# Reordering TensorE, ScalarE and VectorE queues in a Fourier-layer stage and an attention stage

## The chip, the cores and the metric

The kernel runs on one core of a Trainium2 chip. The metric is the device time of one execution in microseconds (us); lower is better. All data is fp32. Engines are called PE (TensorE; PEld is its weight load), DVE (VectorE), ACT (ScalarE), POOL (GpSimd) and SP (the queue that issues most DMAs).

## What is computed

64 images of 64 x 64 x 3 go through a Fourier neural operator, and 64 sequences of 77 text tokens through an embedding; both give rows of 64 numbers, 141 rows for each item. Then come local attention and a two-layer expert MLP over these rows. Cut to what matters:

```python
h = layer_norm(x @ fc0_w + fc0_b, ln0_g, ln0_b)          # 32 channels per pixel
for i in range(4):                                       # four Fourier layers
    x1 = spectral_conv(h, w1, w2)     # rfft2, 12 x 24 modes mixed over channels, irfft2
    x2 = einsum('bchw,oc->bohw', h, conv_w[i]) + conv_b[i]
    h = layer_norm(x1 + x2, ln_g[i], ln_b[i])
    if i < 3: h = gelu(h)
h = gelu(h @ fc1_w + fc1_b); h = gelu(h @ fc2_w + fc2_b); h = h @ fc3_w + fc3_b
h = concatenate([h[..., 0], text_embedding(x_txt)], axis=1)       # 64 + 77 rows of 64
h = h + attention(layernorm(h))        # 8 heads of 8, a 7 x 7 local mask, softmax
h = h + experts(layernorm(h))          # relu MLP, two layers, one of 16 experts by route_id
```

## The kernel before, in words

The images are taken as 32 pairs. `token_network` has a stem (about the first 500 us), three inner layers that run inside a hardware loop over `s` (about 553 to 1038, 1090 to 1590 and 1630 to 2130 us) and a last layer with the heads (to about 3010 us). `attention_and_experts` takes the last 620 us. Each engine has its own program, written out in the order of the source. Engines meet only at semaphores, and an engine waits where its program says so, with everything behind that wait queued.

**Inner layers** (`layer(s)` of each engine). A pair `g` has two halves `h`, and each half two units `u`. On PE, `step(g)` works on up to three pairs at once:

- `widen(s, 0, g, h)` (L479, two matmuls of 512 columns) starts the PSUM banks of half `h` with the inverse transform; it waits for the spectrum copies `zb` of DVE and ACT and for the bank to be read out (`norm_ready`).
- `conv(s, 0, g, h)` (L496, 32 matmuls) adds the 1 x 1 convolution; its end lets ACT square (`square`, L772), DVE sum the squares (`reduce`, L1073), POOL raise them to the power -1/2 (`rstds`, L1296), DVE scale, multiply and add (`normalise` L1087, `gain` L1121, `bias` L1128) and ACT apply gelu (`gelu`, L784, into `hp`).
- `turn(s, 0, g, h, k)` (L546, four transposes of `hp`), copied out by ACT's `hc_copy` (L796) into `ho`, which SP stores.
- `f1(s, 0, g, j)` (L571, 32 matmuls, j = 0 to 3) is the forward transform along x. It writes one PSUM bank, which ACT's `a_copy` (L812) must empty before the next `f1`. `f1` with j = 0 waits for all four gelus of its pair. `f2` (L585) is the transform along y, and ACT's `x_copy` reads it.
- `i1(s, g + 1, first, end)` (L507) is the inverse transform along y of the next pair, in three pieces of 24, 20 and 20 matmuls. Its result is copied by DVE and ACT (`z_copy`, L1133 and L817) into `zb`, for the next `widen`.

PE's loop body is one pair and runs 31 times in each layer; ACT's and DVE's loop bodies hold two pairs, with `even` and `odd` for the two halves. In PE's body before, `widen` of half 0 stands first, so the end of the loop lies between the last `f1` and it, and `f1` with j = 0 follows the second `conv`. In ACT's `odd`, the two squares stand ahead of the four `a_copy`.

**Attention.** A pair has three blocks b = 0, 1, 2, and `step(i, p, b)` of each engine works on up to four pairs. DVE adds the mask to the scores (`with_mask`, L1821), takes the maximum (`row_max`, L1831), POOL subtracts it (`shift`, L1930), ACT takes the exponential (`exp`, L1713), and PE transposes (`turn`, L1581) and multiplies with the values (`values`, L1594). Around it run two layer norms: `norm` (DVE) and `power` (POOL), and `norm_end` (DVE, L1804), the product with the reciprocal deviation: `xn` for the attention's norm of the next pair, `yn` for the experts' norm of the pair before the last. PE transposes `yn` in `back_y` (L1621), ACT copies it (`yT_copy`, L1727), and `exp` is behind `yT_copy` in ACT's queue. POOL's `with_bias` (L1937) writes `h1b`. All of it is at b = 0 of DVE's step:

```python
                if here:
                    with_mask(i, p, b)
                if b == 0 and nxt:
                    norm1_end(*nxt[0:2])
                if here:
                    row_max(i, p, b)
                if b == 0 and (c := at(i, p, 0, 9)):
                    final(*c[0:2])
                if b == 0 and old:
                    norm_end(yn, rs2, rs2_ready, yn_ready, num(old[0], old[1]))
```

Of the kernel before, what the change touches and what calls it, by code (L numbers as in the profile page):

```python
# [25 lines left out]
PAIRS = IMGS // 2  # L26
# [58 lines left out]
def token_network(nc, t, tokens):  # L85


    with ExitStack() as ctx:
# [361 lines left out]
        def _(pe):  # L450
# [157 lines left out]
            def layer(s):  # L608

                def where_older(g):  # L610
                    return nullcontext() if isinstance(g, int) else pe.If(g >= 2)
# [4 lines left out]
                def step(g):  # L616
                    edge = isinstance(g, int)
                    here = not edge or g < PAIRS
                    old, older = not edge or 1 <= g <= PAIRS, not edge or g >= 2
                    if here:  # L620
                        widen(s, 0, g, 0)
                    if older:
                        with where_older(g):
                            turn(s, 0, g - 2, 1, 0)
                    if here:
                        conv(s, 0, g, 0)
                    if older:
                        with where_older(g):
                            turn(s, 0, g - 2, 1, 1)
                            f2(s, 0, g - 2, 0)  # L630
                    if old:
                        turn(s, 0, g - 1, 0, 0)
                    if older:
                        with where_older(g):
                            f2(s, 0, g - 2, 1)
                    if old:
                        turn(s, 0, g - 1, 0, 1)

                    if here:
                        widen(s, 0, g, 1)  # L640
                        conv(s, 0, g, 1)
                    for j, piece in enumerate(((0, 6), (6, 11), (11, 16), None)):
                        if old:
                            f1(s, 0, g - 1, j)
                        if here and piece:
                            with where_next(g):
                                i1(s, g + 1, *piece)
                step(0)
                with pe.Fori(1, PAIRS) as g:
                    step(g)  # L650
# [108 lines left out]
        def _(act):  # L759
# [98 lines left out]
            def layer(s):  # L858
                def even(i, p):
                    here, old, older, nxt = (where(i, p, 0, lag) for lag in (0, 2, 4, -2))  # L860
                    if older:
                        hc_copy(s, older[0], 1, 0)
                    if here:
                        square(s, here[0], 0, 0)
                    if older:
# [15 lines left out]

                def odd(i, p):
                    here, old, nxt = (where(i, p, 0, lag) for lag in (0, 2, -2))
                    if here:
                        square(s, here[0], 1, 0)
                        square(s, here[0], 1, 1)
                    if old:
                        for j in range(4):
                            if j == 3 and nxt:
                                z_copy(s, nxt[0])  # L890
                            a_copy(s, 0, old[0], j)
                    elif nxt:
                        z_copy(s, nxt[0])
                    if here:
                        gelu(s, here[0], 0, 0)
                        gelu(s, here[0], 0, 1)
# [464 lines left out]
def attention_and_experts(nc, t, tokens, out):  # L1361

    with ExitStack() as ctx:
# [122 lines left out]
        def num(i, p):  # L1486
            return 2 * i + p
# [284 lines left out]
        def _(dve):  # L1772
# [109 lines left out]
            def step(i, p, b):  # L1882
                here, prev, old = at(i, p, 0, 0), at(i, p, 0, 3), at(i, p, 0, 6)
                nxt, nxt2 = here and at(i, p, 0, -3), here and at(i, p, 0, -6)
                if here:
                    with_mask(i, p, b)
                if b == 0 and nxt:
                    norm1_end(*nxt[0:2])
                if here:
                    row_max(i, p, b)  # L1890
                if b == 0 and (c := at(i, p, 0, 9)):
                    final(*c[0:2])
                if b == 0 and old:
                    norm_end(yn, rs2, rs2_ready, yn_ready, num(old[0], old[1]))
                if b == 0 and prev:
                    o_norm(*prev[0:2])
                if b == 1 and prev:
# [178 lines left out]
```

## Time and profile before

| | us |
|---|---|
| median of 3 runs | 3648.15 |
| the 3 runs | 3648.17, 3635.49, 3648.15 |
| profiled execution, its time | 3639.14 |
| profiled execution, its span | 3637.3 |
| PE busy | 3132.9 (86%) |
| DVE busy | 2467.3 (68%) |
| ACT busy | 2218.8 (61%) |
| POOL busy | 2127.3 (58%) |
| granted TensorE clock, mean | 0.933 |

The span is the time from the first to the last instruction of the profiled execution; 1.8 us of that execution's time lie around it. The three runs differ by 13 us among themselves, and the profiled one lies between them. The busy shares are means over stages with different limits; for the change only the inner layers and the attention matter.

### The profile page before, as it was taken

The numbers are of one execution on the slowest core, as the hardware profiler recorded it, in microseconds if no ns is written. First come the engines' busy times: TensorE is split into PE (matmuls) and PEld (weight loads), VectorE is DVE, ScalarE is ACT, GpSimd is POOL, SyncE is SP. The second block draws the span as 40 slices with busy tenths as digits, with TensorE's granted clock in tenths as the row PEclk, the third lists the DMA queues.
The fourth block names the chain that finished last, engine by engine and source line by source line (L and its number), as shares of the span: only waits on it lengthen the run. The fifth ranks groups of instructions, "written<-read, shape, count | busy, mean of one in ns | idle before, by whom it ended". The sixth has DMA issues, their size and how long they took to land. (4 is left out here: it accounts for less than half of the span.)

```text
span 3637.3 us, 202203 instructions
## 1 busy us (share of the span) xinstructions
PE 3132.9 (86%) x86496; PEld 2151.1 (59%) x86496; DVE 2467.3 (68%) x3756; ACT 2218.8 (61%) x3645; POOL 2127.3 (58%) x1147
## 2 busy tenths in 40 slices
PE   6777777999968999968999958999999986999998
PEld 3555556777756777756777753333333334666666
DVE  6665547888847888847888844444444436999996
ACT  4455445777745777746777736777777773555554
POOL 2322216888847888838888834444444434555554
PEclk8888887999988999979999978999999997999998
DMA  2232234555544556545555641211121111000000
GB/s 83 94 93 93 88 128 131 169 168 168 172 149 135 169 174 171 171 137 146 168 168 172 174 133 47 60 56 52 54 58 54 54 28 41 13 12 12 12 12 9
DMA packets 206411, 366.15 MB, mean 101 GB/s; under 512 B 107186, under 2 KB 124146, under 8 KB 206018
## 3 DMA queue, kind: packets, MB, share of 16 engines
q1 hardware_dynamic: 194610, 350.25, 32.5%
q10 hardware_dynamic: 7920, 10.03, 0.9%
q0 software_dynamic: 3744, 3.84, 0.7%
q8 instruction: 110, 1.80, 0.2%
q14 instruction: 27, 0.22, 0.0%
HBM read 206.31 MB, written 157.71 MB: 100 GB/s over the span
## 5 line engine op out<-in xcount | busy, mean ns | idle before, releaser
L1296 POOL TENSOR_TENSOR rstd<-var,mhalf 128x16 f32<-128x16 f32 x512 | 1537.4, 3018 | 773.9 <-DVE var L1073 767.2
L571 PE MATMUL ps<-d,hp 128*32 128x48 f32 x32768 | 492.9, 211 | 89.7 <-ACT asb L812 41.7
L571 PEld LDWEIGHTS ps<-d,hp 128*32 128x32 f32 x32768 | 410.2, 112 | 207.6 <-issue 106.3
L1073 DVE TENSOR_REDUCE var<-sq 128x16 f32<-128x528 f32 x384 | 402.8, 1050 | 146.3 <-ACT sq L772 146.2
L812 ACT COPY asb<-ps 128x384 f32<-128x384 f32 x512 | 254.3, 497 | 386.9 <-PE ps L571 264.8
L1087 DVE TENSOR_TENSOR zt<-ps,rstd 128x512 f32<-128x512 f32 x512 | 351.4, 686 | 200.0 <-POOL rstd L1296 195.5
L546 PE MATMUL ps<-ident,hp 128*128 128x128 f32 x2048 | 377.9, 309 | 12.7 <-ACT ho L796 10.0
L496 PEld LDWEIGHTS ps<-cwl,hc 64*64 64x64 f32 x16384 | 273.4, 139 | 146.9 <-issue 136.3
L772 ACT ACTIVATE sq<-ps 128x512 f32<-128x512 f32 x512 | 288.0, 599 | 115.4 <-PE ps L496 81.7
L507 PEld LDWEIGHTS ps<-dyi,gt 64*48 64x48 f32 x16384 | 234.7, 125 | 202.0 <-issue 190.0
L479 PE MATMUL ps<-zb,ex 48*128 48x512 f32 x1024 | 303.5, 668 | 53.8 <-issue 34.8
L507 PE MATMUL ps<-dyi,gt 64*48 64x32 f32 x16384 | 277.2, 212 | 80.7 <-ACT gt L836 36.4
L546 PEld LDWEIGHTS ps<-ident,hp 128*128 128x128 f32 x2048 | 275.7, 197 | 110.3 <-issue 79.2
L1073 DVE TENSOR_REDUCE var<-sql 128x16 f32<-128x528 f32 x128 | 141.2, 1105 | 262.4 <-ACT sql L772 262.4
L496 PE MATMUL ps<-cwl,hc 64*64 64x64 f32 x16384 | 309.2, 226 | 0.0
L920 ACT ACTIVATE a<-ps,fc1b 128x1024 f32<-128x1024 f32 x256 | 271.3, 1111 | 61.1 <-PE ps L689 61.1
L585 PE MATMUL ps<-cy,asb 128*64 128x24 f32 x6144 | 253.1, 222 | 58.2 <-issue 57.4
L705 PE MATMUL ps<-a,fc 128*64 128x512 f32 x1024 | 260.9, 619 | 18.4 <-ACT a L920 18.4
L585 PEld LDWEIGHTS ps<-cy,asb 128*64 128x64 f32 x6144 | 220.0, 143 | 95.7 <-issue 69.9
L1121 DVE TENSOR_TENSOR zt<-zt,gbx 128x512 f32<-128x512 f32 x384 | 264.9, 690 | 10.2
L1128 DVE TENSOR_TENSOR zt<-zt,gbx 128x512 f32<-128x512 f32 x384 | 264.7, 689 | 10.3
L796 ACT COPY ho<-ps 128x512 f32<-128x512 f32 x384 | 223.5, 582 | 72.5 <-PE ps L546 72.5
(171 smaller groups left out, 4881.3 us busy)
## 6 DMA issues: line engine op xcount, KB each, us to landing
h_scratch<-ho SPq DMA_DIRECT2D x256, 512.0 KB
hc<-h_scratch SPq DMA_DIRECT2D x256, 512.0 KB, 4.4
wsb<-in_w SPq DMA_DIRECT2D x64, 288.0 KB
gin<-g_scratch SPq DMA_DIRECT2D x252, 72.0 KB
gin<-g_scratch SPq DMA_DIRECT2D x504, 36.0 KB
g_scratch<-hp SPq DMA_DIRECT2D x32, 192.0 KB, 3.4
g_scratch<-hp ACTq DMA_DIRECT2D x32, 192.0 KB, 4.1
tokens<-wsb SPq DMA_DIRECT2D x256, 4.0 KB
```

Source lines behind the costliest of these rows:

```text
L479: nc.tensor.matmul(main_ps(s, h, u), ex[k], zb[b][k, h, :], start=True, stop=False, skip_group_check=True, tile_position=(64 * u, 0))
L496: last = nc.tensor.matmul(main_ps(s, h, u)[64 * m:64 * m + 64, r:512:8], hc[b][k, 8 * h + r, 64 * m:64 * m + 64], cwl[k], start=False, sto ...
L507: last = nc.tensor.matmul(z[c][64 * u:64 * u + 2 * TRIG, 32 * col:32 * col + 32], gt[b][rows, k].rearrange("k n s a -> k (n s a)"), dyi[ro ...
L546: last = nc.tensor.transpose(t_mid[:, 128 * a:128 * a + 128], src, ident[:])
L571: last = nc.tensor.matmul(a_ps[row:row + 32, 2 * TRIG * k:2 * TRIG * k + 2 * TRIG], hp[b][:, u, 8 * j + k].rearrange("p v r -> p (v r)"), ...
L585: last = nc.tensor.matmul(x_ps[64 * c:64 * c + 64, o:o + KY], asb[b][:, KX * m + 2 * a + c].rearrange("y c s -> y (c s)"), cy[:], start=Tr ...
L772: nc.scalar.activation(dst, main_ps(s, h, u).rearrange("p (v n) -> p v n", v=2), ACT.Square).then_inc(sq_ready, 1)
L920: nc.scalar.activation(a1[:, 2 * u:2 * u + 2, :], f1_ps[:, 2 * u:2 * u + 2, :], ACT.Gelu, bias=fc1b[:]).then_inc(a1_ready, 1)
L1073: nc.vector.tensor_reduce(dst, src, axis=AX.X, op=ALU.add).then_inc(var_ready, 1)
L1087: nc.vector.tensor_tensor(by_px(zt[h][:, u]), by_px(main_ps(s, h, u)), scale, ALU.mult).then_inc(norm_ready, 1)
L1121: nc.vector.tensor_tensor(z, z, channels(s, 0).unsqueeze(2).to_broadcast([128, C, 16]), ALU.mult).then_inc(gain_ready, 1)
L1296: nc.gpsimd.tensor_tensor(rstd[u][:], var[u][:], mhalf[:], ALU.pow).then_inc(rstd_ready, 1)
```

## The change

It moves instructions and removes none. In PE's layer step, `widen` of half 0 goes to the end of the body, for the next pair (for pair 0 it is issued ahead of the loop); `f1` with j = 0 goes ahead of the second `conv`; the first transpose of half 1 (`turn(.., 1, 0)`) goes from the next step to a place ahead of the last `f1`. ACT follows: the first `a_copy` ahead of the squares of half 1, `z_copy` and `hc_copy(.., 1, 0)` ahead of the last `a_copy`. In the attention, DVE's product `yn` goes from behind the maximum of block 0 to right behind the mask.

```diff
--- before.py
+++ after.py
@@ -618,11 +618,6 @@
                     here = not edge or g < PAIRS
                     old, older = not edge or 1 <= g <= PAIRS, not edge or g >= 2
                     if here:
-                        widen(s, 0, g, 0)
-                    if older:
-                        with where_older(g):
-                            turn(s, 0, g - 2, 1, 0)
-                    if here:
                         conv(s, 0, g, 0)
                     if older:
                         with where_older(g):
@@ -638,13 +633,23 @@
 
                     if here:
                         widen(s, 0, g, 1)
+                    if old:
+                        f1(s, 0, g - 1, 0)
+                    if here:
                         conv(s, 0, g, 1)
-                    for j, piece in enumerate(((0, 6), (6, 11), (11, 16), None)):
-                        if old:
-                            f1(s, 0, g - 1, j)
-                        if here and piece:
+                    for j, piece in enumerate(((0, 6), (6, 11), (11, 16))):
+                        if here:
                             with where_next(g):
                                 i1(s, g + 1, *piece)
+                        if old and j == 2:
+                            turn(s, 0, g - 1, 1, 0)
+                        if old:
+                            f1(s, 0, g - 1, j + 1)
+                    if not edge or g < PAIRS - 1:
+
+                        with where_next(g):
+                            widen(s, 0, g + 1, 0)
+                widen(s, 0, 0, 0)
                 step(0)
                 with pe.Fori(1, PAIRS) as g:
                     step(g)
@@ -858,8 +863,6 @@
             def layer(s):
                 def even(i, p):
                     here, old, older, nxt = (where(i, p, 0, lag) for lag in (0, 2, 4, -2))
-                    if older:
-                        hc_copy(s, older[0], 1, 0)
                     if here:
                         square(s, here[0], 0, 0)
                     if older:
@@ -881,16 +884,19 @@
 
                 def odd(i, p):
                     here, old, nxt = (where(i, p, 0, lag) for lag in (0, 2, -2))
+                    if old:
+                        a_copy(s, 0, old[0], 0)
                     if here:
                         square(s, here[0], 1, 0)
                         square(s, here[0], 1, 1)
                     if old:
-                        for j in range(4):
-                            if j == 3 and nxt:
-                                z_copy(s, nxt[0])
-                            a_copy(s, 0, old[0], j)
-                    elif nxt:
+                        a_copy(s, 0, old[0], 1)
+                        a_copy(s, 0, old[0], 2)
+                    if nxt:
                         z_copy(s, nxt[0])
+                    if old:
+                        hc_copy(s, old[0], 1, 0)
+                        a_copy(s, 0, old[0], 3)
                     if here:
                         gelu(s, here[0], 0, 0)
                         gelu(s, here[0], 0, 1)
@@ -1884,14 +1890,14 @@
                 nxt, nxt2 = here and at(i, p, 0, -3), here and at(i, p, 0, -6)
                 if here:
                     with_mask(i, p, b)
+                if b == 0 and old:
+                    norm_end(yn, rs2, rs2_ready, yn_ready, num(old[0], old[1]))
                 if b == 0 and nxt:
                     norm1_end(*nxt[0:2])
                 if here:
                     row_max(i, p, b)
                 if b == 0 and (c := at(i, p, 0, 9)):
                     final(*c[0:2])
-                if b == 0 and old:
-                    norm_end(yn, rs2, rs2_ready, yn_ready, num(old[0], old[1]))
                 if b == 0 and prev:
                     o_norm(*prev[0:2])
                 if b == 1 and prev:
```

On PE, in the inner layers' loop body, the stretch from the second widening on, before (L479 widen, L496 conv, L571 f1, L507 i1, L546 turn):

```order
L479 MATMUL ps<-zb,ex 128x512 x2
L496 MATMUL ps<-cwl,hc 64x64 x32
L564 REGISTER_ALU
L571 MATMUL ps<-d,hp 32x48 x32
L614 COMPARE_AND_BRANCH
L515 ISA
L517 REGISTER_ALU
L507 MATMUL ps<-dyi,gt 48x32 x24
L646 UNCONDITIONAL_BRANCH
L571 MATMUL ps<-d,hp 32x48 x32
```

The same place of the changed kernel:

```order
L479 MATMUL ps<-zb,ex 128x512 x2
L564 REGISTER_ALU
L571 MATMUL ps<-d,hp 32x48 x32
L496 MATMUL ps<-cwl,hc 64x64 x32
L614 COMPARE_AND_BRANCH
L515 ISA
L517 REGISTER_ALU
L507 MATMUL ps<-dyi,gt 48x32 x24
L642 UNCONDITIONAL_BRANCH
L571 MATMUL ps<-d,hp 32x48 x32
```

The first `f1` now stands between the widening and the `conv` of half 1, and a whole `conv` and a piece of `i1` lie between it and the second `f1`.

At the end of PE's body in the changed kernel (L654 is the loop's end):

```order
L546 MATMUL ps<-ident,hp 128x128 x4
L48 REGISTER_ALU
L571 MATMUL ps<-d,hp 32x48 x32
L614 COMPARE_AND_BRANCH
L470 ISA
L476 REGISTER_ALU
L479 MATMUL ps<-zb,ex 128x512 x2
L650 UNCONDITIONAL_BRANCH
L654 REGISTER_ALU
L654 COMPARE_AND_BRANCH
```

Before, the last `f1` was followed by the loop's end; now the next pair's widening lies between them, and the transpose of half 1 ahead of them.

On DVE, block 0 in the attention's loop body, before:

```order
L1821 TENSOR_TENSOR sm<-pst,mask 128x952
L1803 ISA
L1804 TENSOR_TENSOR xn<-xn,rs 128x192
L1831 TENSOR_REDUCE mx<-sm 128x8
L1867 ISA
L48 REGISTER_ALU
L1870 TENSOR_TENSOR fin<-pst,h1b 128x192
L1803 ISA
L1804 TENSOR_TENSOR yn<-yn,rs 128x192
L1835 ISA
L1837 RECIPROCAL rden<-pst 128x24
```

The same place of the changed kernel:

```order
L1827 TENSOR_TENSOR sm<-pst,mask 128x952
L1809 ISA
L1810 TENSOR_TENSOR yn<-yn,rs 128x192
L1809 ISA
L1810 TENSOR_TENSOR xn<-xn,rs 128x192
L1837 TENSOR_REDUCE mx<-sm 128x8
L1873 ISA
L48 REGISTER_ALU
L1876 TENSOR_TENSOR fin<-pst,h1b 128x192
L1841 ISA
L1843 RECIPROCAL rden<-pst 128x24
```

The product `yn` moved ahead of `xn` and of the maximum; the final sum and the reciprocal follow the maximum directly.

## Rows read from the trace of the kernel before

**Rows 1.** Stretches: length, busy and (instructions) of each engine, PEclk, DMA share, GB/s.

```profile
800.00:1037.70 237.70, 221.99 (x9216) 175.80 (x9216) 204.12 (x281) 170.06 (x318) 210.16 (x89) 1.00 0.57 165
...
3320.00:3440.00 120.00, 108.64 (x1259) 81.98 (x1251) 110.18 (x155) 66.28 (x114) 69.31 (x65) 0.97 0.05 12
```

**Rows 2.** Waits, 800 to 1037.7 us: who for whom, total us, times, longest.

```profile
DVE var L1073 <- ACT sq L772: 21.5, 16, 2.0
...
PE ps L479 <- issue: 6.4, 16, 0.4
PE ps L571 <- ACT asb L812: 5.0, 17, 0.9
```

**Rows 3.** Timeline of PE, one pair of layer 1: start, us, what [idle before <- releaser].

```profile
710.80 0.89 PE L571 MATMUL ps<-d,hp 128*32 128x48 f32 x64
...
712.07 1.13 PE L479 MATMUL ps<-zb,ex 48*128 48x512 f32 x4 [0.39 <-issue]
...
713.78 1.16 PE L496 MATMUL ps<-cwl,hc 64*64 64x64 f32 x64
...
719.52 1.16 PE L496 MATMUL ps<-cwl,hc 64*64 64x64 f32 x64
...
720.61 0.89 PE L571 MATMUL ps<-d,hp 128*32 128x48 f32 x64
...
721.70 0.74 PE L507 MATMUL ps<-dyi,gt 64*48 64x32 f32 x48 [0.20 <-issue]
...
722.63 0.89 PE L571 MATMUL ps<-d,hp 128*32 128x48 f32 x64 [0.19 <-ACT asb L812]
...
723.45 0.65 PE L507 MATMUL ps<-dyi,gt 64*48 64x32 f32 x40
...
726.92 1.13 PE L479 MATMUL ps<-zb,ex 48*128 48x512 f32 x4 [0.39 <-issue]
```

**Rows 4.** The same timeline, DVE and ACT behind the first conv.

```profile
715.81 1.05 DVE L1073 TENSOR_REDUCE var<-sq 128x16 f32<-128x528 f32 x1 [1.64 <-ACT sq L772]
...
718.94 0.63 ACT L784 ACTIVATE hp<-zt 128x512 f32<-128x512 f32 x1 [0.44 <-DVE zt L1128]
```

**Rows 5.** Waits in the attention, 3060 to 3600 us.

```profile
PE pst L1621 <- DVE yn L1804: 40.0, 29, 1.6
...
PE pst L1570 <- DVE sm L1821: 6.0, 9, 1.8
```

**Rows 6.** Source line L1804: ns min/median/max, first and last start.

```profile
L1804 DVE TENSOR_TENSOR yn<-yn,rs x30: 341/1881/1890, 3064.4 to 3594.5; 128x192 f32<-128x192 f32 x30
```

**Rows 7.** Timeline of the attention, block 0 of one pair.

```profile
3335.93 1.14 DVE L1821 TENSOR_TENSOR sm<-pst,mask 128x952 f32<-128x952 f32 x1
...
3337.32 0.59 POOL L1937 TENSOR_TENSOR h1b<-h,bo 128x192 f32<-128x192 f32 x1
3337.38 0.74 DVE L1804 TENSOR_TENSOR xn<-xn,rs 128x192 f32<-128x192 f32 x1 [0.31 <-POOL rs L1915]
3338.05 1.13 DVE L1831 TENSOR_REDUCE mx<-sm 128x8 f32<-128x952 f32 x1
...
3338.78 1.10 PE L1594 MATMUL pst<-vv,pT 119*64 119x9 f32 x32
...
3339.26 1.78 POOL L1930 TENSOR_TENSOR sm<-sm,mx 128x952 f32<-128x952 f32 x1 [1.35 <-DVE mx L1831]
3339.37 1.88 DVE L1804 TENSOR_TENSOR yn<-yn,rs 128x192 f32<-128x192 f32 x1
...
3341.39 0.49 PE L1621 MATMUL pst<-identt,yn 128*64 128x128 f32 x3 [1.51 <-DVE yn L1804]
...
3341.92 0.47 ACT L1727 COPY yT<-pst 64x384 f32<-64x384 f32 x1 [2.64 <-PE pst L1621]
...
3342.30 1.00 ACT L1713 ACTIVATE sm<-sm 128x952 f32<-128x952 f32 x1
...
3343.34 1.13 PE L1581 MATMUL pst<-identt,sm 128*119 128x128 f32 x8
```

## The prediction

> **What bounds the kernel now.** I read the page first (busy shares, the 40 slices), then the stretches and the waits of the two stages that the change touches, then one pair of each in the timeline. In the inner layers the 16 pairs of a steady stretch take 237.70 us, 14.86 us each, with PE busy for 221.99 us, POOL for 210.16, DVE for 204.12 and ACT for 170.06 [rows 1]. PE is the bound and stands still for 15.7 us, 0.98 us a pair. That is the ceiling of any gain from order alone: 93 passes of the loop (31 in each of three layers) times 0.98 is 91 us. The waits say where it stands still: 6.4 us in 16 gaps ahead of the widening (L479), and 5.0 us in 17 gaps ahead of f1, for ACT's copy [rows 2]. In the attention PE is the bound too (108.64 of 120.00 us, DVE 110.18) [rows 1]; 40.0 us of its idle time lie in 29 waits for the product yn, 1.38 us each, and only 6.0 us in waits for the mask [rows 5]. The pair there takes 18.28 us, from the first and last start of 30 products (530.1 / 29) [rows 6].
>
> **The layers, part by part.** The matmuls are the same, so I price only gaps.
>
> (a) The widening of half 0. From the last f1 to it 712.07 - 710.80 = 1.27 us pass; from an f1 to the piece of i1 behind it, with a branch but no register wait, 723.45 - 722.63 = 0.82 [rows 3]. So 0.45 us lie in the loop's end and the widening's waits. Behind its new place there is no loop's end, but a branch and the same waits. The nearest row is the first f1 with the first i1, which has a branch and register waits too: 721.70 - 720.61 = 1.09, or 0.27 over 0.82 [rows 3]. I take 0.27 as what stays and 0.18 as the gain. The bounds are 0 (all stays) and 0.45 (nothing stays). The loop's end moves under the widening, which keeps PE busy for 1.13 us [rows 3]; I cost it at nothing, and at up to 0.45 if that cover fails. The spectrum copies it waits for get the transpose and the f1, some 1.5 us, as cover.
>
> The Trainium skill (TensorE: Matmul & The Clock Gate, the table at its head) gives PE a queue of 64 instructions. Read as a sequencer that runs far ahead, that would hide all these waits, (a) would give its full 0.45, and the sum would be 25 us better. The row speaks against it here: the first i1 starts late with "issue" as its releaser, behind an f1 of 64 records [rows 3]. I go by the row.
>
> (b) The second f1. It waits for the first a_copy, which ACT does behind two squares: 0.19 us in the pair shown [rows 3], 5.0 / 16 = 0.31 us in the mean [rows 2]. With the conv (1.09 us from its start to what follows) in between and the a_copy ahead of the squares, this wait goes. Some of the 17 gaps belong to other f1s, so I take 0.25, bounds 0.19 and 0.31.
>
> (c) Gaps at the new neighbours. The conv now stands behind an f1 and the first i1 behind the conv. The i1's 0.27 was there before; the conv's own wait may show as up to 0.27 more. I take 0, since its wait adds no register instruction in the listing.
>
> (d) A new wait. The first f1 needs all four gelus of its pair. The last starts 718.94 - 713.78 = 5.16 us after the first conv, waits for DVE, and takes 0.63 [rows 3, 4]: ready at 5.79, with some 0.05 for the semaphore 5.84. The f1 takes the old place of the second conv, 719.52 - 713.78 = 5.74 [rows 3]. Before, it came at 6.88 and had 1.04 to spare; now it is 0.10 late. I take 0.10, with 0 as the lower bound; upward it is as large as DVE is late (a rival below).
>
> What moves without a price: the second conv starts about 0.85 us later against the first. Its squares had to wait for ACT's copies anyway, and DVE's idle time ahead of the first reduce, 21.5 / 16 = 1.3 us a pair [rows 2], takes what is left. SP's loads of the half that this conv frees, and of the coefficients queued behind them, are issued as much later and are used one pair, over 13 us, later. On ACT the copy hc_copy of half 1 now stands ahead of the last a_copy and the gelus; its transpose comes before the last f1 on PE too, so ACT meets them in PE's order. POOL is busy for 13.1 us of a pair and stays under 14.5.
>
> Sum of the layers: 0.18 + 0.25 - 0.10 = 0.33 us a pair, so 93 x 0.33 = 31 us. At the upper bounds 0.45 + 0.31 = 0.76, 71 us; at the lower 0 + 0.19 - 0.10 - 0.27 = -0.18, a loss of 17 us. The edges of each layer (four passes outside the loop) I leave out.
>
> **The attention.** Before, yn starts at 3339.37, 0.11 us behind POOL's subtraction of the maximum, and lasts 1.88 us, until just after that ends; uncontended it took 0.34 at its shortest [rows 6, 7]. Its input has been ready since before the mask. Now it runs right behind the mask, at about 3337.1, beside POOL's power, an instruction of 3 numbers a row. PE's transpose (L1621) need not wait behind the values (3338.78 + 1.10 = 3339.88), so the wait of 1.51 goes [rows 7]. **Late next** is the exponential: it starts at 3342.30 because yT_copy (3341.92) stands ahead of it, though the subtraction ended at 3339.26 + 1.78 = 3341.04 [rows 7]. It will start at about 3341.1, 1.2 us sooner, and PE's next transposes (3343.34), which need it, come 1.2 us sooner as well; PE itself is there sooner still and waits some 0.3 us for it.
>
> The price is the maximum's start. It was 3338.05, behind xn, which was ready at about 3337.35 and took 0.74 beside POOL's h1b [rows 7]. yn fits into the gap of 0.31 ahead of xn, and xn ends with h1b as before, so I take 0.1 us of delay. Bounds: 0; or all of yn's 0.34 and one more h1b of 0.59, 0.93. Gain: 1.2 - 0.1 = 1.1 us a pair; between 1.2 - 0.93 = 0.27 and 1.38. With 30 products: 33 us, between 8 and 41.
>
> **The sum.** 31 + 33 = 64 us off the profiled execution's 3639.1: 3575 us. The median of the runs shown, 3648.15, is 9 us above that execution, so as a median it may come out a little higher; I say 3576.
>
> **The rivals.** 0.5% of this kernel, 18 us, is about what a measurement can tell from no change.
>
> 1. The layers give nothing, because the gelu wait and gaps at the new neighbours eat (a) and (b); for it speaks that each is no larger than 0.3. Then the attention alone gives 33: 3606 us.
>
> 2. PE's clock rises as well. In the attention the granted clock is 0.97 in the mean, against 1.00 in the steady layers [rows 1]. Of its two levels (1.2 and 2.4 GHz) that means 6% of the time at the lower, 7.2 us of 120, worth up to 3.6 us there and some 16 us over 530. The engine stood still 1.4 us in each pair before it fell. If these falls go, and the layers reach their upper half (50 us): 3639 - 33 - 16 - 50 = 3540 us. The Trainium skill (TensorE: Matmul & The Clock Gate, A second HAM failure mode: psum-queue depth-cycling) says that short idle times between groups of matmuls can make the clock oscillate; by it the falls would go. That the steady layers have idle times and no falls speaks for it only in part.
>
> 3. In the attention, yn and xn both wait for h1b, the maximum comes 0.93 late, and 8 us are left of 33: 3600 us. Against it: yn starts before h1b.
>
> 4. **Slower:** the first f1 waits for a late gelu. DVE does the last half's normalise, gain and bias behind the first reduce, and all PE's work queues behind this f1. From 0.33 + 33 / 93 = 0.68 us beyond the 0.10 on, the whole change loses. If DVE were 1.2 us late in every pair, the layers would lose 93 x 0.87 = 81 us and the total be 3639 - 33 + 81 = 3687 us. Against it: DVE is idle for 1.3 us ahead of that very reduce [rows 2, 4].
>
> 5. The change does less than it says: the product still meets a POOL instruction and the layers' gaps are refilled at once. That is within 18 us of before, say 3630.
>
> **How the numbers follow.** The forecast has 0.63, rival 1 0.15, rival 2 0.10, rival 3 0.04, rival 4 0.04, rival 5 0.04. Faster holds the forecast, rivals 2 and 3 and nearly all of rival 1: 0.90; the same 0.06; slower 0.04. The range reaches down to just below rival 2, 3538, and up past rival 1 to where the layers are at their lower bound and the attention gives its 33: 3639 + 17 - 33 = 3623.
>
> **What would show it.** Right: in a steady layer a pair takes about 14.5 us, the waits for a_copy ahead of f1 nearly vanish, the gap ahead of the widening shrinks to about 0.2, and short waits of the first f1 for gelu appear. In the attention the pair takes about 17.2 us, yn lasts 0.35, and PE's wait for it is gone, with a smaller one for the exponential in its place. Wrong: PE waits for gelu of 0.5 us or more, a gap at the second conv, or a maximum that starts 0.5 us late.

## The result and the profile after

| | before | after |
|---|---|---|
| median | 3647.64 us (4 runs, 3635.49 to 3648.17) | 3548.15 us (4 runs, 3545.62 to 3558.63) |
| profiled execution | 3639.14 us | 3549.24 us |
| its span, mean clock | 3637.3 us, 0.933 | 3547.4 us, 0.937 |

The ratio is 0.9727 (95% interval 0.9704 to 0.975): 2.7% faster, 99.5 us between the medians and 89.9 between the profiled executions. The forecast was 3576 us in a range from 3538 to 3623. The side and the range hold; the gain is larger than the 64 us of the sum.

I cut both spans at three places: the first matmul of the mix (the product of the spectrum with the layer's weights) of the first and of the fourth layer, and the start of the last matmul of the heads' second product (L705, after the change L710). The three inner layers with their mixes take 1611.6 us before (520.3 to 2131.9) and 1562.5 after (520.7 to 2083.2), **49.1 us less** (forecast 31). From that last matmul to the end it is 639.0 and 597.1, **41.9 us less** (forecast 33). The rest changes by 1 us.

The same two kinds of stretch after (columns as in [rows 1]):

```profile
800.00:1030.00 230.00, 218.09 (x9146) 173.92 (x9144) 204.45 (x278) 170.08 (x316) 206.85 (x88) 1.00 0.53 167
3240.00:3360.00 120.00, 115.77 (x1356) 87.61 (x1360) 109.18 (x171) 72.22 (x124) 76.39 (x72) 1.00 0.06 13
```

Against [rows 1], PE is busy for 94.8% of the layers' stretch instead of 93.4%, and for 96.5% of the attention's instead of 90.5%; there the granted clock is now 1.00, where it was 0.97.

**The layers.** A pair takes 14.41 us (mean of the distances between widenings two pairs apart, in eight places) against 14.87: 0.46 less, 43 of the 49.1 us over 93 passes. The other 6 lie in one place near the start of each layer. From the widening of half 1 in pair 1 to that in pair 2 it takes 23.81, 24.35 and 21.96 us in the three layers before, and 21.33, 20.72 and 21.61 after: 6.5 us less together, with a mean granted clock of 0.66, 0.72 and 0.84 there before and of 0.84 in all three after. Not all of it need come from the change: in the experiments below that have before's layers (attention alone, nine matmuls of no use, yn behind xn) the three add up to 68.9 to 72.8 us, in those that have the widening moved to 62.8 to 70.8. The waits after, 790 to 1015 us (columns as in [rows 2]):

```profile
DVE var L1079 <- ACT sq L777: 9.9, 23, 0.5
...
DVE zt L1093 <- POOL rstd L1302: 8.5, 7, 1.2
...
PE ps L571 <- ACT hp L789: 2.5, 8, 0.4
...
PE ps L479 <- DVE zb L1139: 1.9, 8, 0.3
PE ps L479 <- issue: 1.7, 8, 0.2
PEld ps L571 <- ACT asb L817: 0.5, 3, 0.2
```

PE's waits of f1 for asb [rows 2] are gone, those of the widening on "issue" fell from 6.4 us in 16 gaps to 1.7 in 8. Two new ones stand in their place, both 8 times, in every second pair: f1 for the gelu, and the widening for the spectrum's copy zb. DVE now waits up to 1.2 us for POOL's power, in every second pair too. The pairs themselves alternate between about 14.25 and 14.57 us; before, nearly all took 14.8 to 14.95.

The timeline of PE shows where each is, in a pair with these waits and in one without (columns as in [rows 3]):

```profile
698.19 1.13 PE L479 MATMUL ps<-zb,ex 48*128 48x512 f32 x4
699.63 0.89 PE L571 MATMUL ps<-d,hp 128*32 128x48 f32 x64 [0.31 <-ACT hp L789]
700.45 1.16 PE L496 MATMUL ps<-cwl,hc 64*64 64x64 f32 x64
701.66 0.74 PE L507 MATMUL ps<-dyi,gt 64*48 64x32 f32 x48
702.33 0.89 PE L571 MATMUL ps<-d,hp 128*32 128x48 f32 x64
...
705.24 0.71 PE L546 MATMUL ps<-ident,hp 128*128 128x128 f32 x4
705.88 0.89 PE L571 MATMUL ps<-d,hp 128*32 128x48 f32 x64
707.01 1.13 PE L479 MATMUL ps<-zb,ex 48*128 48x512 f32 x4 [0.25 <-DVE zb L1139]
708.07 1.16 PE L496 MATMUL ps<-cwl,hc 64*64 64x64 f32 x64
...
712.75 1.13 PE L479 MATMUL ps<-zb,ex 48*128 48x512 f32 x4
713.93 0.89 PE L571 MATMUL ps<-d,hp 128*32 128x48 f32 x64
```

The first f1 starts 1.44 us behind the widening of half 1 in one pair and 1.18 in the next, where a following matmul without a wait comes at 1.06 (707.01 to 708.07); in both it starts 0.05 us after the last gelu has ended. The conv starts 0.82 behind that f1, the first i1 1.21 behind the conv, the second f1 0.67 behind that i1. The last f1 is followed by the widening of the next pair after 1.13.

**Why every second pair.** POOL and DVE just ahead of the next late pair:

```profile
723.96 0.27 POOL L1312 TENSOR_SCALAR wmean<-wmean 128x18 f32<-128x18 f32 x1
...
724.44 1.16 POOL L1314 TENSOR_TENSOR wsb<-wsb,wmean 128x576 f32 x1 [0.20 <-POOL wmean L1312]
...
725.79 0.67 POOL L1318 TENSOR_TENSOR wsb<-wsb,sgn 128x288 f32 x1 [0.19 <-POOL wsb L1314]
...
726.05 0.95 DVE L1127 TENSOR_TENSOR zt<-zt,gbx 128x512 f32<-128x512 f32 x1
...
726.41 6.25 POOL L1302 TENSOR_TENSOR rstd<-var,mhalf 128x16 f32<-128x16 f32 x2
...
729.91 0.69 DVE L1093 TENSOR_TENSOR zt<-ps,rstd 128x512 f32<-128x512 f32 x1 [1.23 <-POOL rstd L1302]
```

Once in two pairs POOL centres the weights of a coming couple: 2.5 us in three instructions, from 723.96 to 726.46. The two powers rstd come that much later, DVE's normalise waits 1.23 us for one, and DVE's next copies, zb among them, are late. DVE's gain also takes 0.95 us beside the sign product instead of 0.69, ahead of the gelu that f1 waits for. Whether this is what PE waits for is tested below (POOL's centring taken apart).

**The attention.** The product yn after (columns as in [rows 6]):

```profile
L1810 DVE TENSOR_TENSOR yn<-yn,rs x32: 348/348/776, 3014.0 to 3529.7; 128x192 f32<-128x192 f32 x32
```

Its median falls from 1881 to 348 ns. PE's 29 waits for it [rows 5] are gone; what PE still waits for, 3060 to 3500 us, is mainly

```profile
PE pst L1576 <- DVE sm L1827: 7.0, 13, 0.6
...
PE pst L1587 <- ACT sm L1719: 3.3, 18, 0.3
```

and block 0 of one pair reads (columns as in [rows 7]):

```profile
3250.78 1.15 DVE L1827 TENSOR_TENSOR sm<-pst,mask 128x952 f32<-128x952 f32 x1 [0.23 <-issue]
...
3251.85 0.35 DVE L1810 TENSOR_TENSOR yn<-yn,rs 128x192 f32<-128x192 f32 x1
...
3252.12 0.75 DVE L1810 TENSOR_TENSOR xn<-xn,rs 128x192 f32<-128x192 f32 x1
3252.79 1.13 DVE L1837 TENSOR_REDUCE mx<-sm 128x8 f32<-128x952 f32 x1
...
3254.70 0.52 PE L1627 MATMUL pst<-identt,yn 128*64 128x128 f32 x3
...
3255.81 1.00 ACT L1719 ACTIVATE sm<-sm 128x952 f32<-128x952 f32 x1
...
3256.86 1.13 PE L1587 MATMUL pst<-identt,sm 128*119 128x128 f32 x8
```

The maximum starts 2.01 us behind the start of the mask; in the pair of [rows 7] it was 3338.05 - 3335.93 = 2.12. But the pairs alternate, 2.11 and 1.79 before and 2.01 and 2.11 after, and in the mean (21 pairs before, 23 after, 3100 to 3500 us) the maximum starts 1.96 us behind the mask before and 2.06 after: 0.10 later. From the mask to the exponential it takes 5.03 us here where [rows 7] has 6.37, in the mean 5.08 instead of 6.21, so 1.13 less. PE has no wait ahead of its transpose of yn.

### The profile page after: what moved, and what is told of

The parts are those of the page before. It is cut to its first block and busy times, and to the rows that moved or that the text cites. A ratio compares the mean times of both kernels' runs of the same rounds, so it can differ in the third digit from the quotient of the medians.

```text
span 3547.4 us, 202068 instructions
## 1 busy us (share of the span) xinstructions
PE 3109.5 (88%) x86496; PEld 2136.9 (60%) x86496; DVE 2434.8 (69%) x3756; ACT 2229.8 (63%) x3645; POOL 2121.1 (60%) x1147
## 5 line engine op out<-in xcount | busy, mean ns | idle before, releaser
L571 PEld LDWEIGHTS ps<-d,hp 128*32 128x32 f32 x32768 | 412.7, 113 | 288.9 <-issue 128.7
L571 PE MATMUL ps<-d,hp 128*32 128x48 f32 x32768 | 496.9, 212 | 100.2 <-issue 55.9
L546 PE MATMUL ps<-ident,hp 128*128 128x128 f32 x2048 | 375.1, 308 | 11.9 <-ACT ho L801 8.3
L496 PEld LDWEIGHTS ps<-cwl,hc 64*64 64x64 f32 x16384 | 272.1, 139 | 138.4 <-issue 132.2
L507 PEld LDWEIGHTS ps<-dyi,gt 64*48 64x48 f32 x16384 | 232.8, 125 | 176.6 <-issue 164.7
L479 PE MATMUL ps<-zb,ex 48*128 48x512 f32 x1024 | 300.9, 664 | 40.8 <-DVE zb L1139 31.0
L507 PE MATMUL ps<-dyi,gt 64*48 64x32 f32 x16384 | 274.8, 211 | 55.1 <-ACT gt L841 35.2
L496 PE MATMUL ps<-cwl,hc 64*64 64x64 f32 x16384 | 307.7, 226 | 0.0
L546 PEld LDWEIGHTS ps<-ident,hp 128*128 128x128 f32 x2048 | 274.3, 197 | 42.9 <-ACT ho L801 9.0
L1127 DVE TENSOR_TENSOR zt<-zt,gbx 128x512 f32<-128x512 f32 x384 | 275.9, 718 | 10.2
L789 ACT ACTIVATE hp<-zt 128x512 f32<-128x512 f32 x384 | 231.8, 627 | 80.1 <-DVE zt L1134 80.1
L710 PE MATMUL ps<-a,fc 128*64 128x512 f32 x1024 | 261.1, 619 | 18.3 <-ACT a L926 18.3
L1134 DVE TENSOR_TENSOR zt<-zt,gbx 128x512 f32<-128x512 f32 x384 | 265.0, 690 | 10.3
```

Of the source, the lines that this page charges most:

```text
L479: nc.tensor.matmul(main_ps(s, h, u), ex[k], zb[b][k, h, :], start=True, stop=False, skip_group_check=True, tile_position=(64 * u, 0))
L496: last = nc.tensor.matmul(main_ps(s, h, u)[64 * m:64 * m + 64, r:512:8], hc[b][k, 8 * h + r, 64 * m:64 * m + 64], cwl[k], start=False, sto ...
L507: last = nc.tensor.matmul(z[c][64 * u:64 * u + 2 * TRIG, 32 * col:32 * col + 32], gt[b][rows, k].rearrange("k n s a -> k (n s a)"), dyi[ro ...
L546: last = nc.tensor.transpose(t_mid[:, 128 * a:128 * a + 128], src, ident[:])
L571: last = nc.tensor.matmul(a_ps[row:row + 32, 2 * TRIG * k:2 * TRIG * k + 2 * TRIG], hp[b][:, u, 8 * j + k].rearrange("p v r -> p (v r)"), ...
L1127: nc.vector.tensor_tensor(z, z, channels(s, 0).unsqueeze(2).to_broadcast([128, C, 16]), ALU.mult).then_inc(gain_ready, 1)
```

## The experiments

The first four take the change apart. Their comparison has 10 runs of the kernel before, median 3649.22.

**The attention alone.** The two lines of yn moved behind `with_mask` in the kernel before.

> The kernel before with only DVE's product yn moved right behind the mask. The profiles of before and after put 1.30 us a pair and 42 us in all into the attention (pair 18.28 to 16.98 us). If the two parts of the change add up, this gives about 42 us (ratio 0.9885), the clock there is 1.00 instead of 0.96 to 0.97, and the layers stay at 14.86 us a pair. Rival: the parts interact, for instance the attention gains only 33 us (my forecast, order alone, no change of the clock) and the rest came with the layers: ratio 0.991.

Measured: 3599.61 us (4 runs, 3598.84 to 3604.94), ratio 0.9874 (0.9845 to 0.9902). The layers' pair is at its old 14.87 us; the attention's pairs alternate between 16.57 and 17.10, as after the whole change, and the clock is 1.00:

```profile
3150.00:3270.00 120.00, 115.83 (x1380) 87.73 (x1377) 109.27 (x172) 70.62 (x121) 75.98 (x73) 1.00 0.06 13
```

**The layers alone.** The whole change, with yn back behind `final`.

> The changed kernel with yn back behind the maximum: PE's and ACT's part alone. If the parts add up: 49 us (ratio 0.9865), a steady pair of 14.41 us, attention as before with a pair of 18.28 us and falls of the clock. Rival: 31 us, as forecast (0.9915).

Measured: 3596.39 us (4 runs, 3594.45 to 3598.19), ratio 0.9863 (0.9836 to 0.989). The layers' pair is 14.42 us; the attention's is as before, its mean clock too:

```profile
3270.00:3390.00 120.00, 108.34 (x1256) 81.75 (x1253) 109.79 (x159) 64.62 (x111) 68.50 (x67) 0.97 0.05 12
```

0.9874 times 0.9863 is 0.974, within the interval of the whole's 0.9727: no effect of one part on the other is seen, and the rise of the clock belongs to the attention's part.

**Only the first f1 ahead of the conv, its copy ahead of the squares.**

```diff
+                    if old:
+                        f1(s, 0, g - 1, 0)
                     if here:
                         conv(s, 0, g, 1)
...
+                    if old:
+                        a_copy(s, 0, old[0], 0)
                     if here:
                         square(s, here[0], 1, 0)
```

> Before, with only the first f1 ahead of the second conv and the first a_copy ahead of the squares. From the two traces: the wait for a_copy goes (0.26 us a pair), the first i1 stands behind a conv instead of an f1 (0.15 gained), and the first f1 waits for gelu (0.25 lost if the rest of the order were as after). Sum 0.16 us a pair, 15 us, ratio 0.996. In this order the first conv is as late as before, so gelu follows at the same distance (5.84 us behind the first conv) and f1 stands 5.74 behind it: the wait should be 0.10 to 0.25. Rival: the gelu wait eats the part, no gain or a loss (ratio 1.000 to 1.003), and the whole layer gain comes from the widening's part.

Measured: 3631.74 us (7 runs, 3621.13 to 3635.34), ratio 0.9947 (0.9927 to 0.9968); the pair is 14.76 us, 0.11 less. Its waits, 700 to 900 us:

```profile
PEld ps L571 <- ACT hp L787: 11.3, 13, 0.9
...
PE ps L479 <- DVE zb L1138: 8.4, 14, 0.8
...
PEld ps L571 <- ACT asb L815: 2.2, 14, 0.2
```

The waits for asb and gelu fall on PE's weight loads and are mostly hidden behind its matmuls: the first f1 starts 1.17 us behind the widening, 0.11 later than without a wait. But the widening, whose old gap stood on "issue", now waits 0.6 us for the spectrum's copy: PE reaches it earlier and DVE does not. Before, that gap was 0.4 [rows 2], so 0.2 us of what the move gains are given back there, and 0.11 at the f1.

**Only the widening moved**, with the transpose and the loop's body as in the change, f1 and a_copy as before.

> Before, with only the widening of half 0 at the end of the body and the transpose of half 1 ahead of the last f1, ACT's z_copy and hc_copy to match; the first f1 stays behind the second conv. From the two traces: 0.16 us a pair for the gap ahead of the widening and 0.11 for the transpose's neighbours, with no gelu wait: 0.27 us a pair, 25 us, ratio 0.993. Rival: the gap of 0.45 is the loop's jump and shows elsewhere (ahead of the first conv), no gain: 1.000.

Measured: 3610.88 us (4 runs, 3605.87 to 3614.69), ratio 0.9896 (0.9867 to 0.9925). The pair is 14.62 us, 0.26 less, so in the steady part this is what I expected; the time fell more. The three layers with their mixes take 1580.3 us, 31 less, where 93 x 0.26 is 24; the other 7 lie from pair 1 to pair 2 again (20.78, 20.86 and 21.17 us). The two moves by themselves give 0.11 + 0.26 = 0.37, together 0.46. A likely reason is that with the widening at the end of the body its copy has the time that the f1's move alone lacks: the widening's wait for zb is 0.6 us in every pair there, and up to 0.3 in every second pair after the whole change.

The next four ask what limits now, and what the clock was worth. Here the kernel before has 13 runs, median 3649.14.

**The clock by itself.** The kernel before with nine matmuls of no use where PE stood still for yn.

```diff
+                for n in range(9):
+                    nc.tensor.matmul(ps[:, 2, 0:128], ident[:], ident[:], start=True, stop=True)
```

> The kernel before with nine more matmuls of 128 columns on PE, ahead of the transpose that waits for yn, into a PSUM bank that is free there; their result is never read. They take about 1.1 us (eight of their kind take 1.0), so PE is busy where it stood still 1.4 us a pair, and nothing it waits for comes sooner. It asks whether the falls of the clock in the attention (0.96 to 0.97, 1.00 after the change) come from that standstill. If so: clock 1.00 there, the pairs of 19.1 us become 18.0, some 10 us less in all (ratio 0.997). Rival: the clock falls for another reason, and it stays at 0.96 to 0.97; then the pairs of 18.0 us stay or get up to 0.2 us longer (ratio 1.000 to 1.002).

Measured: 3646.27 us (10 runs, 3633.63 to 3650.06), ratio 0.9985 (0.997 to 1.0). In its attention

```profile
3120.00:3240.00 120.00, 119.73 (x1411) 94.92 (x1409) 99.04 (x162) 65.19 (x110) 68.83 (x69) 1.00 0.05 12
```

PE is busy for 99.8% of it and the clock is 1.00 with yn at its old place. But nine took 2.11 us, where I had expected 1.1, more than the gap, so pairs of 18.09 and 18.22 us show only a part of what the clock is worth, and the interval reaches up to no change. I made it again with **five**, in a set of comparisons in which every kernel took about 4.5% less (17 runs of before, median 3481.61; the last section has more on it).

> As the longer filler, with five matmuls instead of nine. Nine took 2.11 us a pair, longer than the 1.4 us of standstill, and gave a granted clock of 1.00 with pairs of 18.09 and 18.22 us; five should take 1.2 us and fit. If the standstill is what lets the clock fall, the clock is 1.00 here too and the pairs are all 17.9 to 18.0 us, none of 19.1: 30 x 0.4 = 12 us less than before, ratio 0.997, with nothing of yn's order changed. Rival: a standstill of 0.2 to 0.3 us with less work in between still lets it fall, and the mean pair stays at 18.3 to 18.4 (ratio 1.000).

Measured: 3471.2 us (12 runs, 3455.92 to 3486.0), ratio 0.9965 (0.995 to 0.998). All its pairs take 17.9 or 18.0 us, none 19.07:

```profile
3020.00:3140.00 120.00, 116.37 (x1343) 89.96 (x1343) 112.19 (x164) 64.93 (x111) 69.46 (x67) 1.00 0.05 12
```

0.35% of this kernel is 12 us (7 to 17 by the interval), and the mean of 27 pairs, 17.95 us instead of 18.41, makes 12 too: the standstill cost its own length and, on top, some 12 us through the clock.

**yn behind xn** instead of ahead of it, in the kernel before: `norm1_end`, then yn, then `row_max`.

> The kernel before with yn between xn and the maximum instead of ahead of both. My theory: the gain comes from taking yn out of POOL's subtraction, and the place ahead of xn is only the cheapest, since DVE waits there for xn's input anyway. Then yn takes 0.35 here and delays the maximum, the subtraction and the exponential by 0.35 to 0.4, against 0.1 in the change: a pair 0.25 to 0.3 us longer than after (17.25 instead of 16.98), gain 31 to 34 us of the attention's 42 (ratio about 0.990). Rival: xn's own end is set by POOL's with_bias, and yn right behind it is held as well or the delay is covered: as good as the change (0.9874) or a loss of more than 0.6 us a pair against it.

Measured: 3604.95 us (4 runs, 3599.04 to 3609.83), ratio 0.9875 (0.9849 to 0.9902); pairs of 16.54 and 16.95, mean 16.75, where I had expected 17.25. My expectation fell, and its rival (as good as the change, 0.9874) came true. The product takes 0.35 us here as well:

```profile
L1804 DVE TENSOR_TENSOR yn<-yn,rs x25: 343/346/346, 3095.0 to 3497.4; 128x192 f32<-128x192 f32 x25
```

What matters is that yn is out from under POOL's subtraction; whether it stands ahead of xn or behind it does not. Both places are ahead of the maximum; one behind it but clear of the subtraction wasn't tried.

**The conv of half 1 split around the first f1**, on the changed kernel, to give the gelu more time (the last argument of `conv` names the half of its matmuls).

```diff
+                    if here:
+                        conv(s, 0, g, 1, 0)
                     if old:
                         f1(s, 0, g - 1, 0)
                     if here:
-                        conv(s, 0, g, 1)
+                        conv(s, 0, g, 1, 1)
```

> The changed kernel with the second conv in two halves of 16 matmuls, the first f1 between them. It gives gelu 0.55 us more and keeps the first a_copy ahead of the squares. If the new wait for gelu (0.38 and 0.12 us in alternate pairs of the changed kernel, 0.25 in the mean) is a loss on PE's path, it goes: a steady pair of 14.16 to 14.2 us instead of 14.41, 20 to 23 us less than the changed kernel (ratio to before about 0.967). Rival: another engine or the spectrum's copy is late next, and the time stays within 5 us of the changed kernel (0.972): the waits ahead of the widening grow by what the f1 gains.

Measured: 3553.51 us (4 runs, 3551.97 to 3557.05), ratio 0.9741 (0.9717 to 0.9764); the pair is 14.44, no less. The wait for the gelu is gone, and the widening waits instead, up to 0.5 us where it was 0.3:

```profile
707.30 1.13 PE L479 MATMUL ps<-zb,ex 48*128 48x512 f32 x4 [0.43 <-DVE zb L1143]
```

So removing the gelu wait alone gives nothing; that both waits hang on the same late DVE is what the experiment after the next tests. The halves also cost 0.08 to 0.26 us more than the conv in one piece.

**The normalise of a new half ahead of the old half's gain on DVE**, on the changed kernel: `z_copy` one line up.

> The changed kernel with DVE's copy of the spectrum ahead of the gain of the same step instead of behind it. In the changed kernel every second widening waits 0.25 us for this copy. If that wait is on the path, 0.12 us a pair goes, 10 us in all (ratio to before 0.970). Rival: it shifts the late gain and bias onto gelu or onto the next reduce, and nothing or a little is lost (0.972 to 0.975).

Measured: 3565.69 us (4 runs, 3564.54 to 3573.25), ratio 0.9771 (0.9749 to 0.9794); the pair is 14.60, 0.19 worse, where I had expected a gain and its rival at most a small loss (0.975). Two of its waits, 790 to 1015 us:

```profile
DVE zt L1093 <- POOL rstd L1301: 15.6, 8, 2.0
PE ps L571 <- ACT hp L789: 4.5, 15, 0.4
```

A DVE that reaches its wait for POOL sooner only waits longer (15.6 us where it was 8.5), and pushes the gain behind it. That points at POOL.

**POOL's centring taken apart.** On the changed kernel, its last product (the sign) is issued one step later, between other powers (`w_sign` is that product, taken out of `w_centre`).

```diff
+                        if p == 1 and h == 0 and not final:
+                            w_sign(s, i)
```

> The changed kernel with the last of POOL's three instructions that centre the next layer's weights (the product with sgn, 0.67 us) put one step later, behind the next pair's first two powers. In the changed kernel these three delay the power of every second pair by about 1 us, DVE waits 1.2 us for it, and the spectrum's copy and the widening behind it come late. If this is what bounds the layers now, DVE's wait falls to about 0.4 us, and the steady pair goes from 14.41 to 14.3 us (the widening's wait of 0.25 in every second pair gone): 10 us less than the changed kernel, ratio about 0.970. Rival: PE is the bound by its gelu wait, and the pair stays at 14.4.

Measured, in the set with before at 3481.61: 3374.34 us (5 runs, 3371.44 to 3385.14), ratio 0.969 (0.9666 to 0.9713). The pair is 14.26 us, 0.16 less than after the change. Its waits, 500 to 700 us:

```profile
PE ps L479 <- issue: 2.9, 14, 0.2
...
DVE zt L1093 <- POOL rstd L1302: 1.3, 7, 0.2
```

DVE's wait for POOL fell from 1.2 us to 0.2, and with it both waits of PE went: the widening's for zb entirely, f1's for the gelu down to 0.12 in every pair. The pairs no longer alternate: nearly all take 14.24 to 14.3 us, what the pairs without the centring took after the change. That settles the cause in the steady pairs. 93 x 0.16 is 15 us; the interval of the ratio just overlaps that of the change, so it is the pairs that show the gain, and not the time.

**The same with the split conv.**

> The same with the second conv in two halves around the first f1. The split alone gave nothing (14.44 us a pair): its gain went into the widening's wait (0.43). If POOL's weights were what held it, the two together give what the split promised: 14.2 us a pair, 20 us less than the changed kernel, ratio about 0.967. Rival: some other engine is late next, and it is no better than e10: 14.3 to 14.4.

Measured: 3376.94 us (5 runs, 3373.61 to 3379.36), ratio 0.9691 (0.967 to 0.9712), a pair of 14.24. I had expected 14.2 us and the pair comes near it, but so does the centring apart by itself (14.26). The split gives nothing here either: the 0.12 of the gelu wait go, and the conv in halves costs about as much.

**The best of both**: the centring apart, and yn behind xn.

> The two best pieces together: the changed kernel with POOL's third weight instruction one step later (14.26 us a pair in the layers, against 14.41) and with yn between xn and the maximum instead of ahead of both (16.75 us a pair in the attention, against 16.84). If both add up: 14.5 and 2.7 us, 17 us less than the changed kernel, ratio to before 0.968. Rival: the place of yn makes no difference beyond the alternation of two pair times, and the ratio is that of the first piece alone, 0.969; the pairs in the attention tell, 16.84 in the mean then.

Measured: 3535.04 us (5 runs, 3527.19 to 3542.73) against 3648.34 (9 runs), ratio 0.9691 (0.9673 to 0.9709). The layers' pair is 14.26, the attention's 16.75. Its median is 13 us below the changed kernel's, where I had expected 17. The ratio is the one of the centring apart by itself; the 0.08 us a pair from yn's place, 2 us in all, is too little for the time to show.

## Why the prediction was right, and where its sum was off

The layers' terms are distances from start to start, means over the 22 pairs between 690 and 1030 us:

| term, us a pair | forecast | measured |
|---|---|---|
| (a) last f1 to widening, 1.29 before | gain 0.18 | 1.11, gain 0.18 |
| (b) second f1, 0.97 before | gain 0.25 | 0.67, gain 0.30 |
| (c) gaps at the conv's new neighbours | 0 | 2.03 (f1 to conv to i1) instead of 2.17 (conv to f1 to i1), gain 0.14 |
| the transpose's neighbours | not in the sum | three gaps, 2.40 before, 2.29 after, gain 0.11 |
| (d) wait for the gelu | loss 0.10 | 1.32 instead of 1.06, loss 0.26 |
| sum of the layers | 0.33 | 0.47, against 0.46 in the pair |
| attention, order alone | 1.1 | 17.96 to 16.82, gain 1.13 |

- **(a)** holds, and **(b)** came out at 0.30, just inside its upper bound of 0.31; the pair of [rows 3] gives 0.26. For (a) the row of the first i1 was the right one to price a branch with register waits by; a PE sequencer that hides them all would have given 0.45 for (a).
- **(c)** was mis-sized at 0, with a loss as its lower bound. The i1's gap shrank from 0.27 to 0.12 behind the conv, and the conv itself stands behind f1 without a gap.
- **The transpose** I moved without pricing its neighbours, though it leaves one place and enters another: 0.11 us.
- **(d)** is the place where the reasoning failed. "POOL is busy for 13.1 us of a pair and stays under 14.5" is a mean; the centring comes in every second pair, in one piece of 2.5 us, and delays the powers in just that pair. By the last experiments that costs 0.16 us a pair; the 0.12 that stays without it is near the 0.10 of the forecast. (The old place of the first f1 was 720.61 - 713.78 = 6.83 us behind the first conv [rows 3] and not 6.88, so it had 0.99 to spare and not 1.04; no term rests on it.) Rival 4 had the right victim, a late DVE, but not its cause. The waits of the kernel before, 800 to 1037.7 us, already show it, at half the length and in every second pair, and I hadn't read that row:

```profile
DVE zt L1087 <- POOL rstd L1296: 4.5, 8, 0.6
```

- **The attention's order** held in both its parts. The maximum is late by the 0.1 that I took, and the exponential starts 1.13 us sooner behind the mask (6.21 to 5.08 in the mean), against 1.2 - 0.1; the pair gains the same 1.13 us. Over the 27 steady distances of the 32 products that is 31 us. I had foreseen a wait of 0.3 for the exponential; its longest is 0.3, and its mean 0.18. What I called the bound there doesn't follow from [rows 1]: DVE was busy for longer than PE, 110.18 of 120 us against 108.64. No run separates the two for the kernel before, since the move both brings yn sooner and takes 1.5 us of work off DVE. For the changed kernel DVE's load isn't the bound: with yn behind xn it is busy for 103.31 of 120 us (3150 to 3270) instead of 109.18, and the pair is nearly the same.
- **The clock**, rival 2, came true. Before, 11 of those 27 distances are about 19.07 us, each with a mean granted clock of 0.91, and the 16 others 17.9 or 18.0, each at 1.00; after, all 27 are at 1.00 and none is longer than 17.2. That is 11 x 1.11 = 12 us, against the 16 that I gave it, and the filler experiment finds the same 12. With 31 + 12 less 1 us at the two ends it makes the 41.9. I gave this rival 0.10 because the steady layers have gaps and no falls; but theirs are several of up to 0.4 us in a pair [rows 3], and here one of about 1.4 (1.51 in [rows 7]) stood in each pair. The Trainium skill (TensorE: Matmul & The Clock Gate, A second HAM failure mode: psum-queue depth-cycling) says that short idle times between groups of matmuls, if they are frequent enough, make the clock go up and down. The attention agrees, as the falls went with the standstill; the steady layers, with idle times in each pair and a clock of 1.00, show that not all short idle times do.
- **The sum.** 43 + 6 at the layers' edges, which I had left out, and 42 for the attention: 91 against 64, less the 1 us of the rest. The medians differ by 9.6 us more than the profiled executions, since before's ran 8.5 us under its median and after's 1.1 above. So the measured 3548 us lies 28 us below the forecast and only 8 above rival 2's 3540, and it lies there for rival 2's two reasons: the falls of the clock went, and the layers gave 49 us, next to its 50. I had given that 0.10. The mechanisms of the forecast were right, but the range held because it had been drawn down to that rival.

## What to carry over

Price a moved instruction at both ends: what stood on either side of its old place, and what stands on either side of the new one. Where an engine's work has a part that comes only in every second or fourth pass, test its cover in the pass where it comes, since a mean over the passes hides it. And an operation that is slow by contention costs where it sits, so it pays to look for a place nearby where the other engine has only small work. Here that was worth 42 us where PE had waited 40 for it; 12 of the 42 came through the clock.

## What was unexpected in the hardware

- **With a standstill of about 1.4 us in each pair of 18** the granted clock was 0.97 in the mean: 11 of 27 pairs had 0.91 and took 1.1 us longer. Filling it with useless matmuls brought 1.00 and took 0.35% off, with everything else as it was.
- **A DVE product with both inputs in SBUF** took 0.35 us alone and 1.88 beside POOL's subtraction of 1.78 us [rows 7], until just after that ended. Beside a POOL power it takes its usual time (0.69 for the gain of 128x512), beside the sign product of the weight centring 0.82 to 0.96. The normalise, which has one input in PSUM, takes 0.68 beside the centring and without it. So "beside POOL" has no single price.
- **The same kernel took 3482 us in one set of comparisons** (17 runs, 3472 to 3496) and 3648 to 3649 in the others. The difference lies ahead of the inner layers: the first mix starts at 361.6 us in the kernel with the centring apart, run there, and at 520.7 in the changed kernel, run in another set. The stretches at the start, of the former and of the latter:

```profile
0.00:350.00 350.00, 313.54 (x10136) 231.18 (x10136) 300.07 (x584) 240.26 (x473) 147.22 (x170) 1.00 0.43 130
```

```profile
0.00:400.00 400.00, 293.80 (x7814) 205.61 (x7815) 240.57 (x475) 189.12 (x369) 116.72 (x136) 0.85 0.29 90
```

The granted clock is 1.00 in the one and 0.85 in the other, and PE is also busy for less of it. Which comes first, and why one set differs, wasn't tried and stays open; the last comparison, in which before takes 3648.34 again, is on record under the same chip number as that set, so the chip alone doesn't explain it; the steady pairs of both agree (14.26 us for that kernel's centring in either set), so the ratios within a set stand.
